# Running products of the high parts ahead of the wait for the low parts in a Perceiver layer on one Trainium2 core

## The reference

```python
def pattention(x, K, V):
    a = softmax(512 ** -0.5 * einsum('btc,nc->btn', x, K))
    return einsum('btn,nc->btc', a, V)

x = x + xattn(ctx, ctx, layernorm(x))           # one head of 64, 25088 keys
h = layer_norm(layernorm(x))                    # 256 x 512
k, q, v = pattention(h, kK, kV), pattention(h, qK, qV), pattention(h, vK, vV)   # 512 keys each
o = causal_sdpa(heads(q), heads(k), heads(v))   # 16 heads of 32
y = pattention(o, pK, pV) + layernorm(x)        # 512 keys
x = x + y + pattention(layer_norm(y), fK, fV)   # 2048 keys
x = x + experts(layernorm(x))                   # top 2 of 8, hidden 1024, silu(h1) * h2
```

## Time and profile before

| | |
|---|---|
| median of 3 runs | 544.38 us (544.32 to 544.78) |
| the profiled execution | 546.02 us |
| its span, first to last instruction | 544.3 us |
| TensorE products (PE) busy | 510.1 us, 94% of the span |
| TensorE weight loads (PEld) busy | 352.6 us |
| VectorE (DVE) busy | 419.0 us |
| ScalarE (ACT) busy | 330.2 us |
| GpSimd (POOL) busy | 37.5 us |
| mean granted clock of TensorE | 0.991 of full speed |

### The profile page before, as it was taken

How to read it: one execution, slowest core, us unless ns; L and a number is a source line. 1 busy time by engine, 2 the same in 40 slices (tenths; PEclk the granted TensorE clock), 3 DMA queues, 4 the chain that set the end, 5 groups by cost and what they waited for, 6 DMA issues and landing times.

```text
span 544.3 us, 11306 instructions
## 1 busy us (share of the span) xinstructions
PE 510.1 (94%) x4324; PEld 352.6 (65%) x4324; DVE 419.0 (77%) x703; ACT 330.2 (61%) x645; POOL 37.5 (7%) x116
## 2 busy tenths in 40 slices
PE   5889999999999999889998989898799999999995
PEld 2434454454445556679766777687688888888885
DVE  2477777877887877778475876998898998998994
ACT  2644554454456454466474547876587788778772
POOL 4000111110110000000312000000000000000000
PEclk9999999999999999899999999998899999999999
DMA  8879989888895700256310303558768987986001
GB/s 317 339 275 387 394 325 338 331 323 321 341 364 181 306 1 4 95 199 220 119 65 8 148 0 138 198 221 306 297 252 289 370 327 255 359 333 209 0 0 43
DMA packets 35939, 122.48 MB, mean 225 GB/s; under 512 B 2609, under 2 KB 2609, under 8 KB 31282
## 3 DMA queue, kind: packets, MB, share of 16 engines
q1 hardware_dynamic: 35602, 121.27, 60.2%
q10 hardware_dynamic: 288, 0.52, 0.3%
HBM read 121.26 MB, written 0.52 MB: 224 GB/s over the span
## 4 chain that ended last, share of the span: by engine, by line
PE 74%; DVE 12%; ACT 5%; issue 3%; ACTq 0%; POOL 0%; DVEq 0%
PE score_banks L1176 15%; PE bank L529 13%; PE bank L1212 7%; PE score_banks L561 7%; PE bank L576 6%; PE score_banks L805 2%; PE bank L545 2%; DVE w_split L2004 2%; PE score_banks L954 2%; ACT xprobs L1258 1%; PE bank L767 1%; PE bank L1185 1%; PE score_banks L978 1%; PE score_banks L1101 1%; PE bank L954 1%
## 5 line engine op out<-in xcount | busy, mean ns | idle before, releaser
L1258 ACT ACTIVATE xprobs<-score_banks,small 128x512 f32<-128x512 f32 (+1 forms) x104 | 67.9, 664 | 88.3 <-DVEq L1723 75.2
L1860 DVE TENSOR_TENSOR w_split<-arena,w_split 128x1024 fp32r<-128x1024 f32 x96 | 114.1, 1222 | 6.1 <-ACT w_split L1413 4.1
L1413 ACT ACTIVATE w_split<-arena 128x1024 fp32r<-128x1024 f32 x96 | 100.7, 1060 | 14.2 <-PE score_banks L1176 9.7
L529 PE MATMUL bank<-arena,wi_sb 128*64 128x512 f32 (+1 forms) x400 | 91.9, 601 | 5.9 <-DMA arena<-in_ctxT 5.9
L1176 PE MATMUL score_banks<-w_split,xg 128*128 128x512 f32 x384 | 88.9, 390 | 1.0 <-ACT xg L1583 1.0
L1732 DVE STREAM_TRANSPOSE xprobsT<-xprobs 128x1024 f32<-128x1024 f32 (+1 forms) x52 | 61.4, 1183 | 33.3 <-ACT xprobs L1258 32.2
L1176 PEld LDWEIGHTS score_banks<-w_split,xg 128*128 128x128 f32 x384 | 71.7, 188 | 16.9 <-ACT xg L1583 1.3
L1704 DVE TENSOR_REDUCE small<-score_banks 128x2 f32<-128x1024 f32 (+1 forms) x52 | 57.3, 1142 | 12.2 <-PE score_banks L561 12.1
L529 PEld LDWEIGHTS bank<-arena,wi_sb 128*64 128x64 f32 x400 | 26.7, 139 | 55.1 <-issue 54.3
L561 PE MATMUL score_banks<-k_full,hT 64*32 64x256 f32 (+1 forms) x1664 | 49.0, 367 | 2.7 <-ACT xprobs L1258 2.6
L1212 PE MATMUL bank<-w_split,hidT 128*128 128x512 f32 x168 | 40.7, 398 | 0.9 <-DVE hidT L2167 0.9
(11 more groups left out here) (339 smaller groups left out, 771.3 us busy)
## 6 DMA issues: line engine op xcount, KB each, us to landing
arena<-in_ctxT SPq DMA_DIRECT2D x24, 2048.0 KB, 8.6
arena<-in_w12T SPq DMA_DIRECT2D x32, 1024.0 KB, 6.0
arena<-in_w3T SPq DMA_DIRECT2D x16, 1024.0 KB, 5.9
arena<-in_fKT SPq DMA_DIRECT2D x4, 1024.0 KB, 7.2
arena<-in_fV SPq DMA_DIRECT2D x4, 1024.0 KB, 5.2
arena<-in_Wo SPq DMA_DIRECT2D x1, 2048.0 KB
arena<-in_ctxT SPq DMA_DIRECT2D x4, 256.0 KB, 5.0
arena<-in_kKT SPq DMA_DIRECT2D x1, 1024.0 KB, 11.7
```

The costliest lines, as they stand in the source:

```text
L529: last = pe.matmul(kp_bank[p][DH * h:DH * (h + 1), 0:half], wi_sb[:, k, :], tokens[:, h * half:(h + 1) * half], start=(k == 0), stop=(k == ...
L1258: act.activation(xprobs[:, qb, 0:2 * width].rearrange("p (h n) -> p h n", h=2), score_banks[:, 2 * p:2 * p + 2, 256 * q:256 * q + width], ...
L1413: act.activation(w_split[:, i % 4, 0, :], raw, ACT.Copy).then_inc(part_high, 1)
L1860: return dve.tensor_tensor(w_split[:, i % 4, 1, :], raw, w_split[:, i % 4, 0, :].bitcast(F32), ALU.subtract)
```

## The change

Five places on TensorE and one on ScalarE; the line numbers of the diff are of the two files.

- `key_scores`: waits for the high part of the activations, issues the eight products with it, then waits for the low part and issues the four with it.
- p scores: feature tiles 0 to 2 as before, but `head_out(3)` now stands ahead of `p_scores(2)`; the last tile (`p_scores_last`) issues four products of the high part after `hT_high` and two of the low part after `hT_done`.
- p rows: `p_rows` replaces `rows_out`; the products with the high part of the probabilities wait only for `key_probsT_high`. Two padding products ahead of the second transposes are taken out.
- f scores: for feature tile 0 of the first half, `f_first` issues the four high products of both banks, then waits for the low part.
- expert 0: of every four weight pieces' first product group, the wait for `xg_low` stands behind the products with the high part.
- ScalarE: the exponential of the second row tile of p ahead of the copy of the first one's transposed probabilities.

```diff
             def key_scores(m, st, bk):
-                pe.wait_ge(ev("hT_done"), ST * TURNS.index("hT") + st + 1)
+                pe.wait_ge(ev("hT_high"), st + 1)
                 split_ready(m + "K")
                 for k in range(KC):
                     w = split_tile(m + "K", k)
-                    for a, (x, y) in enumerate(THREE):
-                        last = pe.matmul(bk, hT_split[x][:, k, st * P:(st + 1) * P], w[y], start=(k == 0 and a == 0),
-                                         stop=(k == KC - 1 and a == 2))
+                    for y in range(2):
+                        pe.matmul(bk, hT_split[0][:, k, st * P:(st + 1) * P], w[y], start=(k == 0 and y == 0), stop=False)
+                pe.wait_ge(ev("hT_done"), ST * TURNS.index("hT") + st + 1)
+                for k in range(KC):
+                    last = pe.matmul(bk, hT_split[1][:, k, st * P:(st + 1) * P], split_tile(m + "K", k)[0], start=False,
+                                     stop=(k == KC - 1))
                 last.then_inc(ev("key_scores"), 1)
...
-                if k < KC - 1:
-                    pe.wait_ge(ev("o_low"), k + 1)
-                else:
-                    pe.wait_ge(ev("hT_done"), ST * TURNS.index("oT") + 2)
+                pe.wait_ge(ev("o_low"), k + 1)
...
+            def p_scores_last():
+
+                w = split_tile("pK", KC - 1)
+                pe.wait_ge(ev("hT_high"), 2 * ST)
+                for st in range(ST):
+                    for y in range(2):
+                        pe.matmul(B[1 + st], hT_split[0][:, KC - 1, st * P:(st + 1) * P], w[y], start=False, stop=False)
+                pe.wait_ge(ev("hT_done"), ST * TURNS.index("oT") + 2)
+                for st in range(ST):
+                    pe.matmul(B[1 + st], hT_split[1][:, KC - 1, st * P:(st + 1) * P], w[0], start=False,
+                              stop=True).then_inc(ev("key_scores"), 1)
+
+            def p_rows(st, bk):
+
+                split_ready("pV")
+                pe.wait_ge(ev("key_probsT_high"), nth("p", st))
+                for n in range(NT):
+                    w = split_tile("pV", n)
+                    for y in range(2):
+                        pe.matmul(bk, ET_split["p"][0][:, n, st * P:(st + 1) * P], w[y], start=(n == 0 and y == 0), stop=False)
+                pe.wait_ge(ev("key_probsT"), nth("p", st))
...
             p_scores(1)
             turn_rsum(3)
+            head_out(3)
             p_scores(2)
-            head_out(3)
-            p_scores(3)
+            p_scores_last()
...
-            keep_awake(SB[0], 2)
             turns_of("p", 1)
             for st in range(ST):
-                rows_out("p", st, B[3 + st])
+                p_rows(st, B[3 + st])
...
+            def f_first(st):
+
+                cols = slice(st * P, (st + 1) * P)
+                for j in range(2):
+                    for y in range(2):
+                        pe.matmul(FB[st][j], hT_split[0][:, 0, cols], w_split[:, 0, y, 512 * j:512 * (j + 1)], start=(y == 0), stop=False)
+                pe.wait_ge(ev("hT_done"), ST * TURNS.index("fT") + st + 1)
+                for j in range(2):
+                    last = pe.matmul(FB[st][j], hT_split[1][:, 0, cols], w_split[:, 0, 0, 512 * j:512 * (j + 1)], start=False, stop=False)
+                if st:
+                    last.then_inc(ev("ffk_used"), 1)
+
             def f_scores(st, half):
-                pe.wait_ge(ev("hT_done"), ST * TURNS.index("fT") + st + 1)
+                pe.wait_ge(ev("hT_high"), 2 * ST + st + 1)
                 for k in range(KC):
                     g = KC * half + k
                     pe.wait_ge(ev("ffk_low"), g + 1)
+                    if half == 0 and k == 0:
+                        f_first(st)
+                        continue
...
                     if first and i % KC == 0:
                         pe.wait_ge(ev("xg_high"), i // KC + 1)
-                        pe.wait_ge(ev("xg_low"), i // KC + 1)
                     pe.wait_ge(part_low, 12 * e + i + 1)
                     w = w_split[:, i % 4]
                     for n, (lhs, part) in enumerate(((x_hi, 0), (x_hi, 1), (x_lo, 0))):
+                        if first and i % KC == 0 and n == 2:
+                            pe.wait_ge(ev("xg_low"), i // KC + 1)
...
             soft_exp("p", 0, B[1])
+            soft_exp("p", 1, B[2])
             probsT_out("p", 0)
-            soft_exp("p", 1, B[2])
             probsT_out("p", 1)
```

More of the change, by code:

```diff
@@ L892, in p_scores @@
                     for a, (x, y) in enumerate(THREE):
[L893 to L896, removed]
+                        pe.matmul(B[1 + st], hT_split[x][:, k, st * P:(st + 1) * P], w[y], start=(k == 0 and a == 0), stop=False)
+            def p_scores_last():
[16 more added lines that the diff above has]
+                pe.wait_ge(ev("key_probsT"), nth("p", st))
+                for n in range(NT):
+                    last = pe.matmul(bk, ET_split["p"][1][:, n, st * P:(st + 1) * P], split_tile("pV", n)[0], start=False,
+                                     stop=(n == NT - 1))
+                last.then_inc(ev("p_out_ready"), 1)
             head_mask(0)
```

## The result

| | before | after |
|---|---|---|
| median of 8 runs | 544.49 us (541.94 to 546.65) | 541.40 us (540.57 to 542.82) |
| ratio, 95% interval | | 0.995 (0.993 to 0.997) |
| the profiled execution | 546.02 us | 540.57 us |
| its span | 544.3 us | 538.8 us |
| mean granted clock | 0.991 | 0.994 |

The change saves 3.1 us by the medians, 1.6 to 3.8 by the interval; 541.7 was forecast, in a range of 540.3 to 543.4. The two profiled executions differ by more, 5.45 us. The timeline of the changed kernel says why. The first fence has one row of VectorE per border between stages: residual of the cross-attention, take_rsum(3), residual of the p stage, first maximum of the second half of the f scores, the flag, the gating product of expert 0.

What follows compares the result with a forecast made beforehand. TensorE's own work was taken as three quarters of the chain, its waits counting only where nothing else is late. Gains of 1.44 + 0.73 + 0.5 = 2.67 us from the median 544.38 gave 541.7 us, range 540.3 to 543.4.

Steps and rivals of the forecast that it cites:

- The k scores at 0: In key_scores: first group starts some 0.7 us earlier, but that wait moves ahead of the q scores; gain 0.
- The p stage: head_out(3) first, 0.81 us earlier, and the second exponential first bring tile 0's residual 1.44 us earlier in all.
- The f scores: In f_first: tile 1's group starts 0.73 us earlier, after ScalarE's copy; tile 0 gains nothing.
- Expert 0: High products start ahead of the gathered tokens' low part: 0.5 us gained, within 0 to 0.66.
- the three falls: Clock at half three times for some 3.4 us, from 220.25, about 367 and 391; forecast holds them as they are.
- rival (a): The clock's fall at 367 goes away as work sits 2.2 us earlier: 1.0 us more, 540.7 us; chance 25%.
- (b): Clock falls ahead of the q scores, their idle stretch grown to 1.8 us: 1.6 us less won, 543.3 us; chance 20%.
- (c): Clock falls ahead of both q scores and p_rows, nothing won at 367: 0.6 us slower, 545.0 us; chance 4%.

## Why the prediction was right, point by point

**The k scores at 0** were right (66.00 to 66.02), and for the reason given: the wait moved ahead of the q scores, to 1.63 us for the 1.8 forecast.

**The p stage** was forecast at 1.44 and measured 1.42. Its steps held, each counted from take_rsum(3): head_out(3) 0.79 us earlier for 0.81, the first maximum 0.69 for 0.73, 0.85 us of idle ahead of the transposes for 1.0. What I said of the split was incomplete. I wrote that p_rows "can start at 299.80, for its high products need only the copy", but not that without it the order on ScalarE gives only 0.30 of its own; and I counted the split of p_scores_last among the steps of the gain, while it delays the first maximum by 0.1.

**The f scores** were forecast at 0.73 for tile 1 and nothing for tile 0: 0.67, all of it lost when the wait is put back. Tile 0's earlier start went into the wait for its second piece, 0.96 us where it was 0.22, as forecast. The low parts of the second half showed no new wait.

**Expert 0** was mis-sized: 0.5 of a range of 0 to 0.66, measured 0.75. Two things failed in that step, and one row was read too widely: the earlier trace rows show the 1.1 us of standing still for VectorE alone, while ScalarE's 4.13 us hold its wait for the flag too. The branch costs TensorE nothing that shows: its products start 2.02 us after the flag's row (370.38 - 368.36), right behind the padding, not 3.16 as before, so the head start is 1.14 us, above the 0.95 that I had called the best. And the bound by VectorE at 1.15 us for each low part was 0.1 us too tight. That VectorE is the bound held: from its first low part behind the flag to the gating product it is busy 14.24 of 14.55 us, before it was 14.60 of 15.31 (by stretch, columns as in the earlier trace rows; after, then before). So 0.4 of the 1.14 us of head start is lost to it.

```profile
369.60:384.15 14.55, 12.15 (x55) 9.48 (x53) 14.24 (x28) 10.44 (x13) 0.00 (x0) 1.00 0.87 333
374.39:389.70 15.31, 12.11 (x55) 9.58 (x53) 14.60 (x28) 10.66 (x13) 0.00 (x0) 1.00 0.78 287
```

**The clock** is where the reasoning failed, though the total hid it. I took the three falls as part of the program ("the chain of numbers above holds the clock as it is") and let rival (a) follow from the shift of the work. Its price was right: 1.0 us forecast, from VectorE's first residual of the f rows to the flag 12.81 us with the fall and 11.69 without, 1.1. Its cause was not: the fall, near 363, is in the traces of two variants of the changed kernel (expert 0 waits for both parts; selections later), and it is missing in those of all five variants of the kernel before. Up to that place these two variants are the changed kernel, instruction for instruction. So one program meets the fall in one execution and not in the next. The Trainium skill (TensorE: Matmul & The Clock Gate, Part 1) states this of the slow products at a kernel's start: what the gate looks at runs free of that start, so their number varies from run to run. The traces agree with it for falls in mid-kernel: the fall at 220 was in the first profile of the kernel before and in two of its variants, and in none of the others. So a spread like that of the kernel before, 541.94 to 546.65, has to be expected, and a sum of terms can be held only against stages, not against one execution.

**Luck.** The sum of the edits was right by stages, 2.67 against 2.82. That the total came out 0.3 us from 541.7 is in part luck: the medians of the kernel before, in the sets of runs taken here, went from 543.77 to 544.59, and the mean clock of its runs from 0.988 to 1.000.

**Rivals (b) and (c)** did not occur: no trace shows a fall between 225 and 300 us, though TensorE stood idle 1.6 us ahead of the q scores in five of them. That gaps bring the clock down was nevertheless right about this kernel in a stretch that the change hardly touches: behind the 3 us idle of expert 0 it fell in all eleven traces that have it. Padding there and in two other places took 2.1 us off the median (541.40 to 539.33, not side by side; the kernel before had 544.49 and 544.59 beside them). Three runs of the changed kernel (542.82 each, clock 0.988) have no trace, so where their falls lay stays open.

## What to carry to other kernels

Splitting a product so that its first part can start ahead of a late operand pays only where TensorE is what the next engine waits for; where another engine's chain ends the stage, the wait just moves, and the order in which that chain is fed (here one group of small products and one exponential) is worth more. Price a change between two borders that no fall of the clock crosses, and look at such stages in both traces before crediting a difference of totals. Before tuning a last microsecond of waits, look whether idle stretches let the clock fall: padding them was worth some 2 us here, where the whole change was worth 3. When a wait is shortened later, shorten its padding too.

## What the runs showed of the hardware

The clock fell after stretches in which TensorE had stood idle or had passed only small products, in some executions of a program and not in others. At half it ran for about 3.4 us, and at expert 0's idle stretch for 3.4 us in seven traces and for 6.8 in four. In the twelve traces without added padding it fell in three near 220 us, behind 1.5 us idle; in three near 365, behind 16 products of eight columns; and in eleven at expert 0's idle stretch of 3 us. It did not fall in the one in which this stretch was 2.0 us, nor ahead of the q scores behind 1.6 us idle, in five traces.

A fall cost 1.1 to 1.6 us ahead of the cross-attention's residual, 1.1 us in the choice of experts, and 1.1 or 2.5 us in expert 0. In the last 3 us it cost nothing, for TensorE had no product left.
